# Five of nine tap products summed with help from Pool, smaller tiles for two matmul stages, and one group of the attention loop for each fill

## The chip, the cores and the metric

One Trainium2 chip, one of its cores. The metric is the device time of one execution in microseconds (us). Engines: PE (TensorE), DVE (VectorE), ACT (ScalarE), POOL (GpSimd, "Pool" below) and SP, which issues the transfers.

## The reference

The input x is 4 images of 64 channels x 64 x 64, float32. Three layers follow one another:

1. A dynamic 3x3 filter. conv1 (64 to 16 channels), batch norm and relu, then conv2 (16 to 9) give nine numbers for each pixel; the output is the sum over the nine taps of shifted pixel times (number + bias): `out = einsum('bckhw,bkhw->bchw', patches, wdyn)`. It is reshaped to (4, 4096, 64): 4096 tokens of 64 an image.
2. `h = h + attention(layernorm(h))`, one head of width 64, softmax over 4096 keys.
3. `h = h + ffn(layernorm(h))`: router logits over 32 experts, the first best one, hidden layer of 16 with relu, back to 64, bias, relu.

## The kernel before, in words

**Tiling.** A block is 1024 queries (8 rows of pixels in each half of an image, 128 partitions x 512 numbers). There are 4 blocks to an image (NQ) and 16 in all (BLOCKS). Attention of block n runs over 16 groups (PAIRS) of 256 keys: in group g, PE multiplies scores for two units (`score`, L573), ACT takes the exponential of each unit (L736), and PE weighs the values of group g-1 (`into_z`, L583) into the PSUM tensor z_ps. Both work in 64x64 tiles, four beside one another.

**Fills.** All other work of PE goes in small steps, "fills", that are laid into the groups of the attention loop by a plan written out by hand (`opening_groups` for n=0 and ahead of it, `second_groups` for n=1, `usual_groups` for n=2 to 15, `last_groups` for n=16). Each fill writes a PSUM bank pair called `both` (the nine taps of block 0 use the two banks of z_ps), and another engine drains it before the next fill may write it. `cc`/`cv` are conv1/conv2 of two blocks at once; SP stores the nine numbers to memory (`store_filters`, L309) and loads them back spread over the 64 channels (`spread_filters`, L321), three taps (a chunk) at a time into two slots. `sum0 sum1 sum2` are DVE's alone: per tap one product (L856, `tap`) and, but for tap 0, one add into hres (L861). Behind the ninth tap DVE normalises the block (L824 to L837, writes `keys`). `xt` turns the keys over (L448), `g` multiplies them by the query-key matrix (L513). Behind attention of block m: DVE adds the two halves of z (L1011, L1013), `pz` multiplies by the value matrix (L521, 128x128 tiles), DVE divides and normalises (L918 to L837, writes y_block), `yt` turns, `lg` gives logits (L527, 128x128 tiles), DVE copies and picks (L928 to L943), `ot` turns the picks, `hid0` to `hid3` are the hidden layer (L539, L543, ACT drains at L729), `o2` the second layer (L550, L556), `fin` turns back (L564) and DVE adds the residual (L954); SP stores the block.

**Order.** In group g, each engine does the scores (or exponentials), then the fills of the group in the plan's order, and PE then weighs group g-1. In a usual block n, with m = n-1 behind and i = n+4 ahead: `sum0` in group 0, `cc` in 1 and `cv` in 5 (for every other n only), `sum1` in 2, `pz` in 3, `sum2` in 4, `yt` in 6, `lg` in 7, `fin` of m-1 in 8, `xt` in 9, `ot` in 10, `hid0` in 11, `hid1` and `g` in 12, `hid2` in 13, `hid3` in 14, `o2` in 15. For n from 12 on nothing lies ahead, so `sum`, `xt` and `g` are missing. n=16 is the tail: only the fills behind block 15, with no attention beside them.

**Opening.** Before the first scores: conv1 of block 0 in full, its nine taps one after another on PE (L473) in 32x128 tiles, each drained by DVE straight from PSUM, with six steps of a bound on the scores' size between them (`pow0` to `pow5`, read by ACT and at last by DVE's `judge`), then the layer norm, `xt`, `cc` of blocks 3 and 4, `g`, `cv`. The sums of blocks 1, 2 and 3 follow on DVE during attention of block 0, whose groups 4, 8 and 12 need the keys of each.

`settle()` is a drain of DVE's pipeline between dependent operations. `rsqrt` is three Newton steps on 128x8 numbers. Pool does only set-up: weights, constants (L360 to L417).

## Time and profile before

| | |
|---|---|
| three timed runs, us | 1240.64, 1241.97, 1242.17 (median 1241.97) |
| the profiled execution, its own time | 1238.29 |
| its span, first to last instruction | 1236.2 |
| mean granted clock of PE | 0.984 of 2.4 GHz |
| PE busy | 1156.3 (94%) |
| ACT busy | 623.8 (50%) |
| DVE busy | 496.5 (40%) |
| POOL busy | 10.1 (1%) |
| chain that ended last, by engine | PE 68%, DVE 20%, waits and queues 12% |

Busy is the time in which at least one instruction of the engine ran. The two largest groups of PE are the scores (L573, 506.1 us busy) and the weighing (L583, 506.6 us), which overlap at their edges. The chain is followed back from the last instruction to what released it at each step. In a timeline, a row gives start, length, engine, line, operation, tiles, count (two records for one float32 matmul), and in brackets how long the engine stood idle before it and which instruction it then followed.

### The profile page before, as it was taken

The page shows a single profiled execution, that of the slowest core. Times are in us where ns is not written, and L with a number is a line of the kernel's source. Part 1 is how long each engine was busy: PE and PEld are TensorE (multiplying, and loading weights), DVE is VectorE, ACT ScalarE, POOL GpSimd, SP SyncE. Part 2 cuts the span into 40 slices and gives each one's busy share as a digit, 9 for nine tenths or more (in the row PEclk, how much of TensorE's full clock was granted, in tenths as well). Part 3 has the DMA queues.
Part 4 walks back from the last instruction along what each step waited for, and adds up shares of the span by engine and source line. Part 5 has one row for each costly group of instructions (what it writes and reads, how often), then busy time and mean ns, then how long its engine had stood idle before and what let it go on. Part 6 is the DMA issues. An engine that isn't in the chain of part 4 may idle for free.

```text
span 1236.2 us, 28064 instructions
## 1 busy us (share of the span) xinstructions
PE 1156.3 (94%) x12122; PEld 464.9 (38%) x12122; DVE 496.5 (40%) x1130; ACT 623.8 (50%) x664; POOL 10.1 (1%) x36
## 2 busy tenths in 40 slices
PE   7698999999999999999999999999999999999965
PEld 2133434333343433434343333434334333434431
DVE  4882774518072452707245170724403030313131
ACT  1255555555555455555555555554555555554611
POOL 3000000000000000000000000000000000000000
PEclk9999999999999999999999999999999999999986
DMA  5543231201214120121212012121000000000000
GB/s 139 120 114 89 70 89 27 63 2 31 57 28 98 27 61 1 32 58 28 60 28 55 10 34 54 27 62 27 10 2 10 1 2 10 1 10 1 10 1 18
DMA packets 11886, 48.42 MB, mean 39 GB/s; under 512 B 2462, under 2 KB 2590, under 8 KB 11372
## 3 DMA queue, kind: packets, MB, share of 16 engines
q1 hardware_dynamic: 11756, 46.53, 15.8%
q8 instruction: 101, 1.65, 0.6%
q14 instruction: 29, 0.24, 0.1%
HBM read 41.77 MB, written 4.75 MB: 38 GB/s over the span
## 4 chain that ended last, share of the span: by engine, by line
PE 68%; DVE 20%; DVEq 4%; issue 4%; ACT 2%; DMA 2%; SPq 0%; ACTq 0%
PE z_ps L583 26%; PE scores L573 24%; PE both L556 5%; DVEq L803 4%; PE both L543 4%; DVE hres L861 4%; DVE tap_product L856 2%; PE both L448 1%; PE z_ps L473 1%; DVE tap_product L828 1%; DVE tap_product L826 1%; DVE stat L824 1%; DVE stat L830 1%; DMA filter_ring<-filters 1%; ACT hidden L729 1%
## 5 line engine op out<-in xcount | busy, mean ns | idle before, releaser
L736 ACT ACTIVATE probs<-scores 128x1024 f32<-128x1024 f32 x480 | 465.4, 1021 | 472.7 <-PE scores L573 472.7
L573 PE MATMUL scores<-g_t,keys_t 64*64 64x512 f32 x4096 | 506.1, 592 | 3.1 <-issue 2.9
L583 PE MATMUL z_ps<-probs,keys 64*64 64x512 f32 x4096 | 506.6, 593 | 0.2 <-DVE z_sb L1013 0.2
L573 PEld LDWEIGHTS scores<-g_t,keys_t 64*64 64x64 f32 x4096 | 170.3, 134 | 281.8 <-issue 275.7
L583 PEld LDWEIGHTS z_ps<-probs,keys 64*64 64x64 f32 x4096 | 160.7, 133 | 230.3 <-issue 204.6
L946 DVE COPY o_sb<-both 128x512 f32<-128x512 f32 x16 | 11.1, 692 | 487.0 <-PE both L556 487.0
L861 DVE TENSOR_TENSOR hres<-hres,tap_product 128x504 f32<-128x504 f32 (+1 forms) x128 | 88.0, 688 | 10.8 <-issue 0.5
L856 DVE SCALAR_TENSOR_TENSOR tap_product<-filter_ring,w,xin 128x504 f32<-128x504 f32 (+1 forms) x120 | 89.0, 742 | 6.1 <-DMA filter_ring<-filters 2.2
L729 ACT ACTIVATE hidden<-both 128x1024 f32<-128x1024 f32 x64 | 65.5, 1023 | 10.0 <-PE both L543 10.0
L543 PE MATMUL both<-y_t,w 64*64 64x512 f32 x512 | 70.0, 618 | 0.0
L556 PE MATMUL both<-hidden,w 64*64 64x512 f32 x512 | 66.2, 604 | 0.0
L736 ACT ACTIVATE probs<-scores,first_scale 128x1024 f32<-128x1024 f32 x32 | 34.1, 1111 | 22.7 <-PE scores L573 22.5
L1011 DVE COPY z_sb<-z_ps 128x512 f32<-128x512 f32 x16 | 11.1, 692 | 81.9 <-PE z_ps L583 81.9
L556 PEld LDWEIGHTS both<-hidden,w 64*64 64x64 f32 x512 | 27.1, 136 | 25.0 <-issue 23.6
L513 PE MATMUL both<-keys_t,a_w 64*64 64x512 f32 x128 | 18.2, 639 | 14.7 <-ACT hidden L729 12.6
L539 PE MATMUL both<-onehot_t,mask_w 64*64 64x512 bf16 x256 | 26.3, 392 | 4.2 <-ACT hidden L729 3.4
L543 PEld LDWEIGHTS both<-y_t,w 64*64 64x64 f32 x512 | 20.2, 138 | 22.7 <-issue 18.9
L564 PE MATMUL both<-w,o_sb 64*64 64x64 f32 x512 | 11.3, 228 | 15.3 <-DVE logits L928 13.6
L725 ACT COPY g_t<-both 128x1024 f32<-128x1024 f32 x16 | 16.2, 1012 | 16.7 <-PE both L513 16.7
L448 PE MATMUL both<-w,keys 64*64 64x64 f32 x512 | 10.9, 225 | 13.8 <-DVE keys L837 13.8
L828 DVE TENSOR_TENSOR tap_product<-tap_product 128x512 f32<-128x512 f32 x32 | 22.2, 693 | 2.4
L830 DVE TENSOR_REDUCE stat<-tap_product 128x8 f32<-128x512 f32 x32 | 22.0, 686 | 2.3
(113 smaller groups left out, 542.9 us busy)
## 6 DMA issues: line engine op xcount, KB each, us to landing
filter_ring<-filters SPq DMA_DIRECT2D x90, 384.0 KB, 5.4
out_dram<-out_sb SPq DMA_DIRECT2D x32, 128.0 KB, 2.4
xin<-x_dram SPq DMA_DIRECT2D x6, 528.0 KB, 7.4
hidden<-once_dram SPq DMA_DIRECT2D x1, 930.0 KB, 12.8
hidden<-once_dram SPq DMA_DIRECT2D x1, 576.0 KB, 4.5
filters<-filters_sb SPq DMA_DIRECT2D x30, 18.0 KB
xin<-x_dram SPq DMA_DIRECT2D x1, 384.0 KB, 6.2
xin<-x_dram SPq DMA_DIRECT2D x1, 368.0 KB, 7.3
```

Source lines behind the costliest of these rows:

```text
L539: T.matmul(both[rows_of(c), r, :], mask_w[rows_of(r), f * 128 + 64 * c:f * 128 + 64 * c + 64], onehot_t[rows_of(r), :], start=True, stop=F ...
L543: last = T.matmul(both[rows_of(c), r, :], w1[rows_of(r), f * 128 + 64 * c:f * 128 + 64 * c + 64], y_t[rows_of(r), :], start=False, stop=True)
L556: last = T.matmul(both[rows_of(r), h, :], w2[rows_of(h), f, :], hidden[rows_of(h), f, r, :], start=(f == 0 and h != r), stop=(f == FT - 1))
L573: last = T.matmul(scores[rows_of(h), c, r * 512:(r + 1) * 512], keys_t[rows_of(r), n // NQ % 2, g * 128 + 64 * h:g * 128 + 64 * h + 64], g ...
L583: last = T.matmul(z_ps[rows_of(c), h, :], keys[rows_of(h), n // NQ % 2, 2 * g + r, :], probs[rows_of(h), (2 * g + c) % RING, r * 512:(r + ...
L729: A.activation(hidden[:, int(name[3:]), :, :], both[:, :, :], ACT.Relu).then_inc(done, 1)
L736: A.activation(probs[:, unit % RING, :], scores[:, c, :], ACT.Exp, scale=SCALE if n else first_scale[:, 0:1]).then_inc(probs_ready, 1)
L803: dve.drain()
L828: V.tensor_tensor(squares[:, :, :], centred[:, :, :], centred[:, :, :], ALU.mult)
L830: V.reduce_sum(total, squares[:, :, :], AX_X)
L856: product = V.scalar_tensor_tensor(dst, flt, keep["b2c"][:, t:t + 1], pix, ALU.add, ALU.mult)
L861: V.tensor_tensor(mine[:, :, lo:hi], mine[:, :, lo:hi], dst, ALU.add)
```

## The change

- **Pool sums.** Tap 2's product goes into a new tile pool_sum; the products of taps 3 to 6 go into two buffers in turn, and Pool adds each to pool_sum. DVE waits before a product whose buffer is still to be read, and, behind tap 8, for all four adds of the block, and then adds pool_sum to hres itself. On DVE five adds a block go and one comes. Pool does `add_products(0)` before the rest of its set-up, and the other blocks' after it.
- **Tiles.** `pz` and `lg` go in 64x64 tiles; ACT instead of DVE drains `lg`. The division behind `pz` is one reciprocal instead of two.
- **Groups.** `fin` of m-1 moves from group 8 to 2, `cv` from 5 to 4, `xt` from 9 to 8, `g` from 12 to 9: each fill has a group of its own. In n=1, `xt`, `g` and `sum2` likewise, and `g` of block 5 moves into n=2. `cc` and `cv` of blocks 3 and 4 move out of the opening into groups 1 and 2 of n=0.
- **Opening.** Six PSUM places for the taps of block 0; tap t uses rows 32(t%4) onward of the array, the six first ones go before `cc`/`cv`; the `pow` steps go behind all taps; DVE's small work on row means moves from tap 0 to tap 6; ACT loads its table before the first data are there.
- **Tail.** For block 15, `hid1`, `hid2` and `o2` get PSUM places of their own, and DVE drains one half of each `hid` (a relu as max with 0) while ACT drains the other.

```diff
+POOL_FIRST, POOL_ADDS = 2, (3, 4, 5, 6)
+PLACE_OF_TAP = (4, 0, 1, 2, 3, 5, 6, 7, 8)
...
 def opening_groups():
-
+    first = "tap0 tap1 tap2 tap3 tap4 tap5"
     return {
-        -1: [*at(0, "c1 tap0 tap1 pow0 aw tap2 pow1 tap3 pow2"), *at(1, "cc"), *at(0, "tap4 pow3 tap5 pow4"),
-             *at(1, "cv"), *at(0, "tap6 pow5 tap7 tap8 xt"), *at(3, "cc"), *at(0, "g"), *at(3, "cv")],
+        -1: [*at(0, "c1 " + first), *at(1, "cc cv"),
+             *at(0, "tap6 tap7 tap8 pow0 aw pow1 pow2 pow3 pow4 pow5 xt g")],
         0: at(1, "sum0 sum1 sum2"),
+        1: at(3, "cc"),
+        2: at(3, "cv"),
         3: at(1, "xt"),
         4: [*at(1, "g"), *at(2, "sum0 sum1 sum2")],
...
-    return {3: at(m, "pz"), 6: at(m, "yt"), 7: at(m, "lg"), 8: at(m - 1, "fin"), 10: at(m, "ot"),
+    return {2: at(m - 1, "fin"), 3: at(m, "pz"), 6: at(m, "yt"), 7: at(m, "lg"), 10: at(m, "ot"),
             11: at(m, "hid0"), 12: at(m, "hid1"), 13: at(m, "hid2"), 14: at(m, "hid3"), 15: at(m, "o2")}
...
-    return merged({1: at(j, "cv"), 0: at(i, "sum0"), 2: at(i, "sum1")}, behind(0),
-                  {4: at(i, "sum2"), 8: at(j, "sum0 sum1"), 9: at(i, "xt"), 12: at(i, "g"), 13: at(j, "sum2"),
-                   16: at(j, "xt g")})
+    return merged({0: at(i, "sum0"), 1: at(j, "cv"), 2: at(i, "sum1"), 4: at(i, "sum2")}, behind(0),
+                  {8: [*at(i, "xt"), *at(j, "sum0 sum1")], 9: at(i, "g"), 12: at(j, "sum2"), 16: at(j, "xt")})
 
...
-    pair = at(j, "cc"), at(j, "cv")
-    ahead = {1: pair[0], 5: pair[1]} if j in PAIRED else {}
-    return merged(ahead, {0: at(i, "sum0"), 2: at(i, "sum1"), 4: at(i, "sum2")}, behind(n - 1),
-                  {9: at(i, "xt"), 12: at(i, "g")})
+    ahead = {1: at(j, "cc"), 4: at(j, "cv")} if j in PAIRED else {}
+    return merged({0: at(NQ + 1, "g")} if n == 2 else {}, ahead,
+                  {0: at(i, "sum0"), 2: at(i, "sum1"), 4: at(i, "sum2")}, behind(n - 1),
+                  {8: at(i, "xt"), 9: at(i, "g")})
...
+                    k = FIRST_TAP + int(name[3:]) % TAP_PLACES if name.startswith("tap") else USUAL
+                    if i == BLOCKS - 1:
+
+                        k = LAST.get(name, USUAL)
...
+        score_banks = [scores[:, c, :].rearrange("p (u n) -> p u n", u=2) for c in range(2)]
+        place = [both, *(score_banks[c][:, u, :] for c in range(2) for u in range(2)), z_ps[:, 0, :], z_ps[:, 1, :],
+                 *score_banks, z_ps]
...
+            def add_products(i):
+                for k, t in enumerate(POOL_ADDS):
+                    nth = i * len(POOL_ADDS) + k
+                    lo, hi = columns_of(t)
+                    pool.wait_ge(product_ready, nth + 1)
+                    P.tensor_tensor(pool_sum[:, :, lo:hi], pool_sum[:, :, lo:hi], pool_product[:, nth % 2, :, lo:hi],
+                                    ALU.add).then_inc(product_added, 1)
+                    pool.drain()
...
+            for i in range(1, BLOCKS):
+                add_products(i)
...
-                    T.matmul(scores[0:DB, 0, 0:DB], centred_qk[:, 0, :], centred_qk[:, 1, :], start=True,
+                    wait_drained("tap4@0")
+                    T.matmul(z_ps[0:DB, 0, 0:DB], centred_qk[:, 0, :], centred_qk[:, 1, :], start=True,
...
-                    T.matmul(mine, load["w2c"][0:32, t * 128:(t + 1) * 128], conv1_first[:, :], start=True,
+
+                    rows = slice(32 * (t % 4), 32 * (t % 4) + 32)
+                    T.matmul(mine, load["w2c"][rows, t * 128:(t + 1) * 128], conv1_first[rows, :], start=True,
                              stop=True).then_inc(done, 1)
...
-                    for p in range(2):
-                        for j in range(2):
-                            jj = 2 * p + j
-                            last = T.matmul(both[:, p, j * 130:(j + 1) * 130], z_sb[:, jj * 128:(jj + 1) * 128],
-                                            wv_w[:, :], start=True, stop=True)
+                    for j in range(BT // 2):
+                        for c in range(2):
+                            for h in range(2):
+                                last = T.matmul(both[rows_of(h), c, j * 65:(j + 1) * 65],
+                                                z_sb[rows_of(c), j * 128 + h * 64:j * 128 + h * 64 + 64],
+                                                wv_w[rows_of(c), c * 65:(c + 1) * 65], start=True, stop=True)
...
-                        last = T.matmul(mine[:, j * 64:(j + 1) * 64], y_t[:, j * 128:(j + 1) * 128],
-                                        router_w[:, :], start=True, stop=True)
+                        for r in range(2):
+                            for h in range(2):
+                                last = T.matmul(both[rows_of(h), r, j * E:(j + 1) * E],
+                                                y_t[rows_of(r), j * 128 + h * 64:j * 128 + h * 64 + 64],
+                                                router_w[rows_of(r), :], start=True, stop=True)
...
+                    if i == BLOCKS - 1 and f == FT - 1:
+                        pe.wait_ge(upper_hidden, 1)
...
+                        if i == BLOCKS - 1:
+                            pe.wait_ge(upper_hidden, f + 1)
...
+                elif name == "lg":
+                    A.copy(logits[:, :, :].rearrange("p (j r) e -> p r j e", r=2),
+                           both[:, :, 0:BT // 2 * E].rearrange("p r (j e) -> p r j e", e=E)).then_inc(done, 1)
...
-                    A.activation(hidden[:, int(name[3:]), :, :], both[:, :, :], ACT.Relu).then_inc(done, 1)
+
+                    mine_of = slice(0, 1 if i == BLOCKS - 1 else 2)
+                    A.activation(hidden[:, int(name[3:]), mine_of, :], mine[:, mine_of, :], ACT.Relu).then_inc(done, 1)
...
+            act.wait_ge(constants_ready, 1)
+            A.activation(table_loaded[:, :], ones[0:1, 0:1], ACT.Relu)
...
+            def first_best(i):
+
+                dve.wait_ge(drained[places.of[f"lg@{i}"]], places.nth[f"lg@{i}"])
...
-                dst = mine if t == 0 else tap_product[:, t % 2, :, lo:hi]
+                if t == 0:
+                    dst = mine
+                elif t == POOL_FIRST:
+
+                    dst = pool_sum[:, :, :]
+                elif t in POOL_ADDS:
+                    nth = i * len(POOL_ADDS) + t - POOL_ADDS[0]
+                    dst = pool_product[:, nth % 2, :, lo:hi]
+                    if nth > 1:
+                        dve.wait_ge(product_added, nth - 1)
+                else:
+                    dst = tap_product[:, t % 2, :, lo:hi]
                 product = V.scalar_tensor_tensor(dst, flt, keep["b2c"][:, t:t + 1], pix, ALU.add, ALU.mult)
                 if sources_free is not None:
                     product.then_inc(sources_free, 1)
                 settle()
-                if t:
+                if t in POOL_ADDS:
+                    V.engine_nop().then_inc(product_ready, 1)
+                elif t and t != POOL_FIRST:
                     V.tensor_tensor(mine[:, :, lo:hi], mine[:, :, lo:hi], dst, ALU.add)
+                if t == TAPS - 1:
+                    dve.wait_ge(product_added, (i + 1) * len(POOL_ADDS))
+                    settle()
+                    V.tensor_tensor(mine, mine, pool_sum[:, :, :], ALU.add)
 
             def judge():
...
+                if name == "lg":
+                    first_best(i)
+                    return
+                if name.startswith("hid") and i == BLOCKS - 1:
+                    f, k = int(name[3:]), places.of[full]
+                    dve.wait_ge(filled[k], places.nth[full])
+                    V.tensor_scalar(hidden[:, f, 1, :], place[k][:, 1, :], 0.0, None, ALU.max).then_inc(upper_hidden, 1)
+                    return
...
                 if full == "tap0@0":
                     dve.wait_ge(x_first_loaded, 32)
+                if full == "tap6@0":
...
-                    sums = both[:, :, 0:260].rearrange("p u (j a w) -> p u j a w", j=2, a=2)
-                    rs = stat[:, 4, :].rearrange("p (u j a) -> p u j a", u=2, j=2)
-                    rows = h2[:, i % 2, :, :].rearrange("p (u j a) w -> p u j a w", u=2, j=2)
-                    for u in range(2):
-                        V.reciprocal(rs[:, u], sums[:, u, :, :, D])
-                        settle()
-                        last = V.tensor_tensor(rows[:, u], sums[:, u, :, :, 0:D], wide(rs[:, u], D), ALU.mult)
+                    sums = both[:, :, 0:BT // 2 * 65].rearrange("p a (j w) -> p a j w", w=65)
+                    rs = stat[:, 4, :].rearrange("p (a j) -> p a j", a=2)
+                    rows = h2[:, i % 2, :, :].rearrange("p (j a) w -> p a j w", a=2)
+                    V.reciprocal(rs, sums[:, :, :, D])
+                    settle()
+                    for a in range(2):
+                        last = V.tensor_tensor(rows[:, a], sums[:, a, :, 0:D], wide(rs[:, a], D), ALU.mult)
                     last.then_inc(done, 1)
```

## Rows read from the trace of the kernel before

**Rows 1.** Windows: span, then busy us (instructions) by engine, granted clock, DMA.

```profile
960.00:1040.00 80.00, 79.76 (x836) 31.45 (x832) 13.67 (x35) 44.75 (x47) 0.00 (x0) 1.00 0.02 5
...
1200.00:1210.00 10.00, 5.39 (x108) 4.73 (x112) 3.54 (x9) 1.17 (x2) 0.00 (x0) 0.50 0.06 15
```

**Rows 2.** Timeline, DVE, two attention blocks; columns: start, us, engine, line, operation, idle before.

```profile
417.30 0.69 DVE L1011 COPY z_sb<-z_ps 128x512 f32<-128x512 f32 x1 [3.69 <-PE z_ps L583]
...
423.98 0.68 DVE L861 TENSOR_TENSOR hres<-hres,tap_product 128x504 f32<-128x504 f32 x1
424.58 0.74 DVE L856 SCALAR_TENSOR_TENSOR tap_product<-filter_ring,w,xin 128x504 f32<-128x504 f32 x1
...
446.75 0.68 DVE L837 TENSOR_TENSOR keys<-tap_product,stat 128x504 f32<-128x504 f32 x1
...
450.53 0.75 DVE L954 SCALAR_TENSOR_TENSOR out_sb<-both,h 128x256 f32<-128x256 f32 x2
...
499.60 0.18 DVE L918 RECIPROCAL stat<-both 128x4 f32<-128x4 f32 x1 [0.68 <-PE both L521]
```

**Rows 3.** Timeline, PE, the first of those two blocks.

```profile
447.82 0.69 PE L564 MATMUL both<-w,o_sb 64*64 64x64 f32 x32 [1.83 <-DVE logits L928]
...
466.48 1.09 PE L513 MATMUL both<-keys_t,a_w 64*64 64x512 f32 x8 [1.14 <-ACT hidden L729]
```

**Rows 4.** Timeline, PE, a late block, where no later block is prepared.

```profile
995.77 1.90 PE L573 MATMUL scores<-g_t,keys_t 64*64 64x512 f32 x16
...
998.68 1.95 PE L583 MATMUL z_ps<-probs,keys 64*64 64x512 f32 x16
...
1009.50 1.90 PE L583 MATMUL z_ps<-probs,keys 64*64 64x512 f32 x16
1011.22 1.90 PE L573 MATMUL scores<-g_t,keys_t 64*64 64x512 f32 x16
...
1014.08 1.95 PE L583 MATMUL z_ps<-probs,keys 64*64 64x512 f32 x16
```

**Rows 5.** Timeline, DVE and POOL in the opening.

```profile
13.39 0.74 DVE L856 SCALAR_TENSOR_TENSOR tap_product<-z_ps,w,xin 128x504 f32<-128x504 f32 x1 [0.96 <-PE z_ps L473]
13.54 0.23 POOL L394 CAST b_bf<-b_rest 32x64 bf16<-32x64 f32 x1
14.23 0.68 DVE L861 TENSOR_TENSOR hres<-hres,tap_product 128x504 f32<-128x504 f32 x1
14.33 0.67 POOL L398 CAST b_bf<-b_rest 32x64 bf16<-32x64 f32 x1
...
19.55 0.41 POOL L408 TENSOR_TENSOR wv_w<-hidden 128x130 f32<-128x130 f32 x1 [2.40 <-DMA hidden<-once_dram]
19.58 0.92 DVE L861 TENSOR_TENSOR hres<-hres,tap_product 128x504 f32<-128x504 f32 x1
...
21.14 1.26 POOL L413 TENSOR_TENSOR w<-hidden 128x512 f32<-128x512 f32 x1
```

**Rows 6.** Timeline of the opening, and the page's line of filter loads.

```profile
14.23 2.07 PE L473 MATMUL z_ps<-conv_first,hidden 32*128 32x512 f32 x2
...
41.71 0.68 DVE L837 TENSOR_TENSOR keys<-tap_product,stat 128x504 f32<-128x504 f32 x1
...
52.56 4.69 PE L573 MATMUL scores<-g_t,keys_t 64*64 64x512 f32 x24
...
55.36 31.56 SPq L321 DMA_DIRECT2D filter_ring<-filters  x12
...
101.96 0.68 DVE L837 TENSOR_TENSOR keys<-tap_product,stat 128x504 f32<-128x504 f32 x1
...
filter_ring<-filters SPq DMA_DIRECT2D x90, 384.0 KB, 5.4
```

**Rows 7.** Timeline, PE, behind the last attention block.

```profile
1213.44 0.64 PE L539 MATMUL both<-onehot_t,mask_w 64*64 64x512 bf16 x4 [1.14 <-ACT hidden L729]
...
1223.94 0.64 PE L550 MATMUL both<-onehot_t,b_parts 64*64 64x512 bf16 x2 [1.15 <-ACT hidden L729]
```

More of the change, by code:

```diff
@@ L295, in store_block @@
                 fin = f"fin@{m}"
[L296 removed]
+                sp.wait_ge(drained[places.of[fin]], places.nth[fin])
                 for half in range(HH):
@@ L461, in fill @@
                 wait_free(full)
-                k = banks_of.sem[full]
-                mine, done = banks[k], filled[k]
+                k = places.of[full]
+                mine, done = place[k], filled[k]
                 par, q = i // NQ % 2, i % NQ
@@ L698, in drain @@
                     act.wait_ge(a_written, 1)
-                    A.copy(a_w[:, :], scores[:, 1, 0:128]).then_inc(a_ready, 1)
+                    A.copy(a_w[:, :], z_ps[:, 1, 0:128]).then_inc(a_ready, 1)
                 if name.startswith(NONE) or not name.startswith(MINE):
                     return
-                k = banks_of.sem[full]
-                mine, done = banks[k], drained[k]
+                k = places.of[full]
+                mine, done = place[k], drained[k]
                 turned = both[:, :, 0:BT // 2 * 64].rearrange("p h (j n) -> p h j n", n=64)
```

154 lines of the change are left out of this document (74 added, 80 removed).

## The prediction

> **What bounds the kernel now.** I read the windows first, then PE's timeline of one block, then DVE's. In a late block PE is busy for 79.76 of 80 us at the full 2.4 GHz level, DVE for 13.67 [rows 1]: PE's own work is the bound there, and only work taken off PE counts. In the blocks that prepare a later one it is not. There PE stands 1.83 us before `fin`, because the bank still holds logits that DVE copies only after it has normalised the keys (end 447.43, copy, `fin` at 447.82), and 1.14 us before `g`, which shares its group with `hid1` and waits for ACT [rows 3]. In these blocks DVE's chain from the copy of z (417.30) to the end of the keys (447.43) is 30.1 us long [rows 2] and sets when PE leaves group 8. Behind the last attention block PE works for 5.39 of 10 us with granted clock 0.50, the 1.2 GHz level [rows 1]: a chain of fills and drains. The opening is a DVE chain too: keys of block 0 at 42.39, of block 3 at 102.64, so 20.1 us for each block between [rows 6].
>
> The sum is made against the profiled execution, 1238.3 us (span 1236.2 and 2.1 around it). The median of the runs is 1242.0, so it lies 3.7 higher, and so I place the forecast. What can be told from no change is about 0.2%, 2.5 us.
>
> **Pool's adds (n=2 to 11).** The question is whether they run beside DVE. Pool's cast of 32x64 takes 0.23 us beside a DVE product that reads PSUM, but 0.67 when it starts 0.10 us into a DVE add of two SBUF tensors, and ends 0.09 behind that add; and a DVE add that begins inside a Pool operation takes 0.92 instead of 0.68 [rows 5]. So they shut each other out, at least in large part. A Pool add of this size is 1.26 us (L413) [rows 5]. DVE's two read-from-SBUF operations are most of what it does in `sum`.
>
> The Trainium skill (SBUF — State Buffer, SBUF: two separate sides) says that a GpSimd operation and a DVE operation with two SBUF inputs lock each other out for the whole instruction. By it four adds would cost 4 x 1.26 = 5.0 us of DVE's time a block wherever DVE had such work. The trace agrees in kind, not quite in size: DVE lost 0.24 us to 0.38 of overlap, 0.63 of it, which would make the four adds 3.2 us.
>
> DVE's chain in such a block, change by change:
> - five adds go, each worth 0.60, the step from its start to the next product [rows 2]: -3.0;
> - one add of pool_sum with its drain comes: +0.8;
> - `fin`'s drain (0.75, L954 [rows 2]) moves ahead of `pz`: +0.75; one reciprocal of 0.18 and its drain go: -0.25;
> - tap 3's add: DVE waits for it before tap 5, 1.26 and some 0.15 of signalling: +1.4;
> - adds of taps 4 and 5: between 0 (they lie beside the drains of `fin` and `pz`, which read PSUM, and beside DVE's wait for `pz`) and 2.6 (Pool gets in before DVE's products, and `fin`, then `pz`, come late); nearest to the first by where they fall: +1.0;
> - tap 6's add falls between products of two SBUF tensors: 1.26, taken as +1.3.
>
> Together +2.0: keys later, not earlier. `xt` now stands in group 8 where `fin` was, so PE waits there for the keys: about 0.2 behind them, at 449.6 where `fin` began at 447.82 before: +1.8. Against this one fill of 0.5 fewer follows (`fin` is done in group 2), and `g` no longer waits (-1.14). Net +0.1. The time saved on `pz` and `lg` is no gain here, since PE waits in group 8 anyhow. In every other block (those with `cc`, `cv`) DVE had waited 0.68 for `pz` [rows 2], which absorbs as much of the +2.0, and PE stood there for less before; with the rest of the same sum about -1.1. Ten blocks: **-5 us**. n=1 likewise: 0. Without any exclusion only the wait of 0.6 before tap 5 remains of the Pool terms, the chain is 1.1 shorter, less what `pz` lets through, and each block gains 2.7: -27. With every add at its worst (+1.6 more) the ten blocks give +11.
>
> **Late blocks (n=12 to 15).** `pz` takes 998.68 - 995.77 - 1.72 = 1.19 us and `lg` 1014.08 - 1011.22 - 1.72 = 1.14, where 1.72 is the step of 16 records of scores or values [rows 4]. In 64x64 tiles each is 16 matmuls, like a turning fill, about 0.5; `fin`, also of 16, is 0.69 with its tail [rows 3]. -0.7 and -0.7, and each had 0.05 of change-over behind it. **-5.8** for four blocks; if the narrower `lg` is quicker still, -6.5. `fin` moved to group 2 costs nothing: DVE is free then. Its place is used again by `pz` one group later, DVE's drain (0.75) lies beside 3.4 us of scores and values.
>
> **Opening.** Before, PE makes a tap in 2.07 us at the low clock [rows 6] and DVE waits 0.96 for it [rows 5]. With six places and four row groups I take four taps in the time of one: two rounds (4 us), `cc`/`cv` with ACT between (5.5), a third round (2). DVE's keys of block 0 then come at about 31, `judge` behind them, and block 1 starts at 32.6 instead of 42.6 (0.2 behind the keys); first scores at 36.5 instead of 52.56. But SP's queue is in order: `store_filters(3)`, then block 2's loads, issued at 55.36 before [rows 6]. `cv` of block 3 is now in group 2, behind two groups' exponentials, drained at about 49. The loads go out at 50.5 and take 5.4 each [rows 6]: block 2 starts at 56 instead of 62.7 (-6.7), and waits 2 us more for its second chunk. Within a block the third chunk can be loaded only when the first is used, and comes 8.8 us after the block's start with fewer adds as with more, so those saved before it give nothing; Pool's adds around it cost about 2 us in each of two blocks. **-1 us** of the 10 that block 1 gains. Without exclusion -5. No trace here shows 32-row tiles beside one another; if they go one by one, keys 0 come only 2 us earlier, the loads of block 2 land at 65, and the opening gives +6.5.
>
> **Tail.** The hidden fills come every 3.50 us, from 1213.44 to 1223.94 [rows 7], and 1.15 of each is PE's wait for ACT. With places of their own they follow one another: 4 x 1.15 = -4.6. PE then has no gaps, and I expect it to reach the 2.4 GHz level before `o2`: between 0 and -4.5, taken as -2.5. `fin` of block 14 goes from between `lg` and `ot` (0.75 of DVE) to under `pz`, which it delays by 0.75; `lg` at the low clock saves 0.8 and `ot` no longer follows `fin`: together about -1.9. **-9 us** (-6 to -11).
>
> **Sum.** -5 - 0 - 5.8 - 1 - 9 = -21: 1217 for a profiled execution, 1220 for the median.
>
> **The rivals.**
> - *Pool's adds are hidden* (0.18). Then -27 - 2 (n=1) - 5.8 - 5 - 9 = -49: 1193. For it: DVE lost less than the full overlap; against it: all three crossings in [rows 5].
> - *Pool's add is the slow link* (0.12). On 8 rows of 63 in a running kernel, with its wait, drain and signal, it may take longer than the 1.26 of a plain 128x512. About three of four adds are on DVE's chain in each of ten blocks, n=1 and two of the opening. From 0.55 us more for each, 1.8 in all, the gain of 21 is used up; at 2.5 us (twice) the sum is -21 + 13 x 3 x 1.24 = +27: 1269. Against it: the one clean row.
> - *Row tiles don't overlap* (0.10): opening +6.5 instead of -1, 1228.
> - The sum as above (0.60): 1220, own range 1207 to 1232.
>
> Faster by over 0.2% is 0.83: the sum, hidden adds, row tiles. Within 0.2%: 0.05, slower 0.12, both from the slow link. The range reaches down to the hidden adds' 1193 and up past the row tiles' case: 1192 to 1240.
>
> **What would show it.** Right: DVE operations of two SBUF inputs stretched or held off beside Pool's adds; Pool busy about 64 x 1.26 = 81 us; PE idle 1 to 4 us before `xt` in each block to n=11 with keys as releaser, none before `fin` and `g`; `pz` and `lg` steps of 0.5; hidden fills of the tail without gaps; block 2's first product after a DMA wait. Wrong: no wait before `xt` (adds hidden, or DVE chain shorter), Pool adds well above 1.3 us, late blocks no shorter, or PE stalls before `pz` for `fin`'s drain longer than 1.3 us.

## The result, and the profile after

The changed kernel takes **1224.46 us** (1223.57 to 1224.93), the kernel before 1241.5 in the same session: a ratio of 0.9861, 95% interval 0.9841 to 0.9880. A fourth execution took 1981.72 us at a mean granted clock of 0.567; it counts in this median, which is 1223.99 without it, but not in the range or the ratio. The forecast was 1220. The profiled execution took 1224.93, with a span of 1223.1 where it was 1236.2 before: 13.1 shorter. The medians differ by 17.0, more than the spans, since the profiled execution of before (1238.29) lay 3.2 under that kernel's median; what follows compares the two traces.

I cut both spans at DVE's copies of z (L1011 before, L1078 after), one at the end of each attention block:

| stretch (us) | before | after | difference | predicted |
|---|---|---|---|---|
| start to z of n=0, and n=1 | 200.81 | 204.21 | +3.4 | -1 |
| n=2 to 11, ten blocks | 720.83 | 721.38 | +0.6 | -5 |
| n=12 to 14 | 201.48 | 196.92 | -4.6 | -4.4 |
| n=15 and the tail | 113.08 | 100.59 | -12.5 | -10.5 |

So the four rows add up to -13 instead of -21. The stretches without Pool's adds gave what was forecast or more, those with them 10 us less.

First the page after: busy time of each engine, PE's granted clock in 40 slices (tenths of full speed), three groups of instructions.

```profile
PE 1130.4 (92%) x12890; PEld 478.8 (39%) x12890; DVE 467.2 (38%) x1038; ACT 626.6 (51%) x681; POOL 114.8 (9%) x98
...
PEclk9989899999999999999999999999999999999996
...
L377 POOL TENSOR_TENSOR pool_sum<-pool_sum,pool_product 128x504 f32<-128x504 f32 x64 | 104.2, 1628 | 750.0 <-DVEq L931 744.9
L469 PE MATMUL both<-w,keys 64*64 64x64 f32 x512 | 15.2, 277 | 54.6 <-DVE keys L879 54.6
...
L933 DVE TENSOR_TENSOR hres<-hres,tap_product 128x504 f32<-128x504 f32 (+1 forms) x48 | 46.9, 976 | 3.9
```

Pool's 64 adds take 1.63 us in the mean, not 1.26. DVE's own add (L933) takes 0.98 in the mean where one took 0.68 [rows 2]. PE stands 54.6 us before `xt` (L469), and one record of `xt` takes 277 ns in the mean.

DVE and POOL in the steady block that answers to [rows 2], where before the same chain ran from 417.30 to 447.43 (timeline; start, us, engine, line, operation, idle before):

```profile
421.43 0.69 DVE L1078 COPY z_sb<-z_ps 128x512 f32<-128x512 f32 x1 [3.69 <-PE z_ps L616]
...
427.18 1.79 POOL L377 TENSOR_TENSOR pool_sum<-pool_sum,pool_product 128x504 f32<-128x504 f32 x1 [54.79 <-DVEq L931]
429.01 0.74 DVE L926 SCALAR_TENSOR_TENSOR pool_product<-filter_ring,w,xin 128x504 f32<-128x504 f32 x1 [1.15 <-POOL pool_sum L377]
...
441.16 1.82 POOL L377 TENSOR_TENSOR pool_sum<-pool_sum,pool_product 128x504 f32<-128x504 f32 x1 [8.86 <-DVEq L931]
441.93 1.60 DVE L933 TENSOR_TENSOR hres<-hres,tap_product 128x512 f32<-128x512 f32 x1
...
451.78 0.68 DVE L879 TENSOR_TENSOR keys<-tap_product,stat 128x504 f32<-128x504 f32 x1
```

The chain is 452.46 - 421.43 = 31.0 us, 0.9 longer than before. DVE waits 1.15 for Pool's first add, and an add of DVE that meets one of Pool's takes 1.60.

PE behind the same keys, then in the next block, answering to [rows 3]:

```profile
452.61 1.13 PE L469 MATMUL both<-w,keys 64*64 64x64 f32 x32 [3.05 <-DVE keys L879]
453.49 3.05 PE L616 MATMUL z_ps<-probs,keys 64*64 64x512 f32 x16
456.35 1.90 PE L606 MATMUL scores<-g_t,keys_t 64*64 64x512 f32 x16
...
525.03 0.69 PE L469 MATMUL both<-w,keys 64*64 64x64 f32 x32 [2.20 <-DVE keys L879]
525.51 1.93 PE L616 MATMUL z_ps<-probs,keys 64*64 64x512 f32 x16
527.23 1.93 PE L606 MATMUL scores<-g_t,keys_t 64*64 64x512 f32 x16
```

and the windows around both (span, busy us of PE, PEld, DVE, ACT, POOL, granted clock, DMA share, GB/s):

```profile
452.00:456.00 4.00, 3.39 (x48) 1.81 (x52) 2.83 (x7) 0.59 (x1) 0.00 (x0) 0.57 0.00 0
...
524.00:528.00 4.00, 2.97 (x56) 1.62 (x60) 3.17 (x8) 0.59 (x1) 0.00 (x0) 1.00 0.02 4
```

Behind the wait of 3.05 us the granted clock is 0.57, so mostly the 1.2 GHz level: `xt` and the weighing take 456.35 - 452.61 = 3.74 us where behind the wait of 2.20 they take 527.23 - 525.03 = 2.20. In this pair **1.5 us are lost to the clock**, on top of the wait; waits of 3.05 to 3.42 stand in every block without `cc` and `cv`. The waits before `fin` and before `g` are gone, as forecast.

A late block's `pz`, answering to [rows 4]:

```profile
998.65 1.90 PE L606 MATMUL scores<-g_t,keys_t 64*64 64x512 f32 x16
1000.37 0.64 PE L545 MATMUL both<-wv_w,z_sb 64*64 64x65 f32 x32
1000.83 1.90 PE L616 MATMUL z_ps<-probs,keys 64*64 64x512 f32 x16
```

From scores to weighing it is 2.18, so `pz` costs 2.18 - 1.72 = 0.46.

The opening, PE's taps of block 0, then SP's queue and DVE's first product of block 2, answering to [rows 6]:

```profile
8.57 2.09 PE L497 MATMUL scores<-conv_first,hidden 32*128 32x512 f32 x8 [1.02 <-ACT conv_first L745]
...
32.34 0.68 DVE L879 TENSOR_TENSOR keys<-tap_product,stat 128x504 f32<-128x504 f32 x1
...
50.80 1.35 SPq L320 DMA_DIRECT2D filters<-filters_sb  x4
52.26 2.37 SPq L332 DMA_DIRECT2D filter_ring<-filters  x4
...
58.33 0.75 DVE L926 SCALAR_TENSOR_TENSOR hres<-filter_ring,w,xin 128x512 f32<-128x512 f32 x1 [3.24 <-DMA filter_ring<-filters]
...
100.52 0.68 DVE L879 TENSOR_TENSOR keys<-tap_product,stat 128x504 f32<-128x504 f32 x1
```

Four taps (8 records) take 2.09 us, where one took 2.07 before. Keys of block 0 come 9.4 us earlier, keys of block 3 only 1.4 earlier. And then PE, at the change from n=0 to n=1:

```profile
118.67 1.90 PE L616 MATMUL z_ps<-probs,keys 64*64 64x512 f32 x16
122.95 1.93 PE L606 MATMUL scores<-g_t,keys_t 64*64 64x512 f32 x11 [2.38 <-issue]
125.99 1.12 PE L606 MATMUL scores<-g_t,keys_t 64*64 64x512 f32 x3 [1.11 <-issue]
...
126.92 3.61 PE L616 MATMUL z_ps<-probs,keys 64*64 64x512 f32 x12
```

From 124 to 131 us the granted clock is 0.55, so PE works mostly at the low level (12 records in 3.61). Before, a stop of 2.20 at this place was followed by full speed (granted clock 1.00 from 120 to 130 us), and z was copied at 128.39 instead of 131.50.

The tail, answering to [rows 7]:

```profile
1206.21 0.64 PE L570 MATMUL both<-onehot_t,mask_w 64*64 64x512 bf16 x4 [0.79 <-ACT onehot_t L764]
1206.61 1.95 PE L574 MATMUL both<-y_t,w 64*64 64x512 f32 x8
...
1208.74 1.73 PE L574 MATMUL scores<-y_t,w 64*64 64x512 f32 x8
...
1212.88 3.61 PE L589 MATMUL z_ps<-hidden,w 64*64 64x512 f32 x30
```

No gaps between the hidden fills; the full clock is back in the second hidden fill (8 records in 1.73 where the first has 1.95, and 30 in 3.61 for `o2`).

### The profile page after: what moved, and what is told of

It reads as the page before. It is cut to its first block, busy times and chain, and to the rows that moved or that the text cites. A ratio compares the mean times of both kernels' runs of the same rounds, so it can differ in the third digit from the quotient of the medians.

```text
span 1223.1 us, 29732 instructions
## 1 busy us (share of the span) xinstructions
PE 1130.4 (92%) x12890; PEld 478.8 (39%) x12890; DVE 467.2 (38%) x1038; ACT 626.6 (51%) x681; POOL 114.8 (9%) x98
## 4 chain that ended last, share of the span: by engine, by line
issue 61%; PE 26%; POOLq 9%; DVE 3%; DVEq 0%; POOL 0%; DMA 0%; ACT 0%
PE z_ps L616 10%; PE scores L606 10%; POOLq L379 8%; PE both L574 2%; PE both L589 1%; PE both L469 1%; PE both L570 0%; PE z_ps L589 0%; PE both L545 0%; DVEq L845 0%; PE both L554 0%; PE both L597 0%; PE scores L574 0%; DVE hres L933 0%; DVE tap_product L870 0%
## 5 line engine op out<-in xcount | busy, mean ns | idle before, releaser
L616 PE MATMUL z_ps<-probs,keys 64*64 64x512 f32 x4096 | 521.0, 605 | 0.5 <-issue 0.2
L606 PEld LDWEIGHTS scores<-g_t,keys_t 64*64 64x64 f32 x4096 | 181.6, 135 | 277.4 <-issue 266.9
L616 PEld LDWEIGHTS z_ps<-probs,keys 64*64 64x64 f32 x4096 | 173.4, 137 | 227.2 <-issue 198.3
L1013 DVE COPY o_sb<-both 128x512 f32<-128x512 f32 x15 | 10.4, 692 | 469.5 <-PE both L589 469.5
L377 POOL TENSOR_TENSOR pool_sum<-pool_sum,pool_product 128x504 f32<-128x504 f32 x64 | 104.2, 1628 | 750.0 <-DVEq L931 744.9
L469 PE MATMUL both<-w,keys 64*64 64x64 f32 x512 | 15.2, 277 | 54.6 <-DVE keys L879 54.6
L768 ACT ACTIVATE hidden<-both 128x1024 f32<-128x1024 f32 (+1 forms) x62 | 62.6, 1010 | 3.0 <-PE both L574 3.0
L926 DVE SCALAR_TENSOR_TENSOR pool_product<-filter_ring,w,xin 128x504 f32<-128x504 f32 x60 | 45.3, 756 | 32.7 <-POOL pool_sum L377 17.3
L933 DVE TENSOR_TENSOR hres<-hres,tap_product 128x504 f32<-128x504 f32 (+1 forms) x48 | 46.9, 976 | 3.9
L1078 DVE COPY z_sb<-z_ps 128x512 f32<-128x512 f32 x16 | 11.1, 692 | 85.0 <-PE z_ps L616 85.0
L755 ACT COPY keys_t<-both 128x512 f32<-128x512 f32 x16 | 9.4, 587 | 59.2 <-PE both L469 59.2
L469 PEld LDWEIGHTS both<-w,keys 64*64 64x64 f32 x512 | 12.9, 181 | 67.5 <-issue 66.7
L926 DVE SCALAR_TENSOR_TENSOR tap_product<-filter_ring,w,xin 128x504 f32<-128x504 f32 (+1 forms) x45 | 33.4, 742 | 3.0
```

The lines of the kernel that those rows point to most:

```text
L377: P.tensor_tensor(pool_sum[:, :, lo:hi], pool_sum[:, :, lo:hi], pool_product[:, nth % 2, :, lo:hi], ALU.add).then_inc(product_added, 1)
L469: last = T.matmul(both[rows_of(a), h, j * 64:(j + 1) * 64], tiles[2 * j + a][rows_of(h)], ident[rows_of(h), rows_of(h)], start=True, stop= ...
L606: last = T.matmul(scores[rows_of(h), c, r * 512:(r + 1) * 512], keys_t[rows_of(r), n // NQ % 2, g * 128 + 64 * h:g * 128 + 64 * h + 64], g ...
L616: last = T.matmul(z_ps[rows_of(c), h, :], keys[rows_of(h), n // NQ % 2, 2 * g + r, :], probs[rows_of(h), (2 * g + c) % RING, r * 512:(r + ...
L768: A.activation(hidden[:, int(name[3:]), mine_of, :], mine[:, mine_of, :], ACT.Relu).then_inc(done, 1)
L926: product = V.scalar_tensor_tensor(dst, flt, keep["b2c"][:, t:t + 1], pix, ALU.add, ALU.mult)
```

## The experiments

Two questions: what do Pool's adds cost, and where did the 8 us go. In the first theory Pool was neutral (it costs DVE about what it takes off DVE); its rivals were that its adds are a net loss or a net gain. A time that is given as so much below or above the changed kernel is against its 1224.46.

**Pool out.** DVE adds all eight products itself.

```diff
-                if t in POOL_ADDS:
-                    V.engine_nop().then_inc(product_ready, 1)
-                elif t and t != POOL_FIRST:
+                if t:
...
-                    V.tensor_tensor(mine, mine, pool_sum[:, :, :], ALU.add)
```

> The changed kernel, but DVE adds all eight products itself again and Pool adds none. Theory A (Pool's adds and DVE's operations on two SBUF tensors shut each other out, so that the adds taken off DVE come back as waits and stretched operations): DVE's chain from the copy of z to the end of the keys stays within 0.5 us of the 31.0 us that it has with Pool, the blocks n=2 to 11 stay as long as they are, and the opening gains some 2 us; 1219 to 1226 us, ratio to the kernel before 0.984 +- 0.003. Rival B (Pool relieves DVE, the loss lies elsewhere): the chain gets 2 us longer, each of ten blocks too, 1240 us or more, ratio about 1.0.

Measured 1205.92 (ratio 0.9719, 0.9702 to 0.9735): 18.5 below the changed kernel. Both expectations missed. Yet the chain from z to keys, by the ten blocks n=2 to 11, is 31.3 us in the mean against 31.5 with Pool and 30.4 before: Pool is neutral for DVE there, and the ten blocks are still 10.6 us shorter, 9.1 of it between the end of the keys and the next copy of z. Another 11.6 us go before z of n=1, and there Pool is not neutral: keys of block 3 come 65.1 us after those of block 0 without it, 68.2 with it. The trace of n=5, the block of the first pair above:

```profile
416.15 0.70 PE L542 MATMUL both<-wv_w,z_sb 64*64 64x65 f32 x32 [1.47 <-DVE out_sb L1004]
...
437.18 0.69 PE L466 MATMUL both<-w,keys 64*64 64x64 f32 x32 [2.23 <-DVE keys L876]
437.67 2.74 PE L613 MATMUL z_ps<-probs,keys 64*64 64x512 f32 x12
```

Without Pool, DVE comes later to `fin`'s drain, so PE stands 1.47 before `pz` (0.26 with Pool) and then only 2.23 before `xt`. The same idle time is cut in two, and `xt` takes 0.69. This block is also the exception: right behind `xt` the clock falls even so (0.60 granted from 437 to 441 us), and it takes 41.3 from keys to the next copy of z. In the nine others that is 39.6 to 39.9, with waits of 1.0 to 2.2 before `xt`. In the changed kernel it is 39.6 behind four of the five waits of 2.2 to 2.6, and 40.9 to 42.5 behind the fifth of them and behind all five of 3.05 to 3.42. That made the clock the new theory.

**`xt` one group later**, with Pool and without (`xt` in group 9, `g` in 16).

```diff
-                  {8: at(i, "xt"), 9: at(i, "g")})
+                  {9: at(i, "xt"), 16: at(i, "g")})
```

> The changed kernel with xt in group 9 instead of 8 and g in group 16 instead of 9, for n=2 to 15. Theory A (what ate the gain is PE's wait for the keys in group 8, 2.2 to 3.4 us in each of ten blocks, and the lower clock behind the longer of these waits, about 1.5 us in every other block): one group later (3.4 us) the wait is gone and the granted clock stays high there; 10 x 2.75 + 5 x 1.5 = 35 us less, about 1190, ratio 0.958. Rival B (DVE's chain bounds the block wherever xt stands: PE waits for the picks before ot, or before pz): less than 10 us gained, ratio above 0.978.

> Both edits: xt in group 9, g in 16, and no adds on Pool. Theory A (Pool's adds are neutral for DVE's chain): within 4 us of the kernel with xt later and Pool's adds, rather below it through the opening; 1184 to 1192 us. Rival B (Pool's adds are what makes room for DVE): over 5 us slower than that kernel, waits before xt come back.

Measured 1196.64 with Pool (0.9636, 0.9620 to 0.9652), 27.8 less where the theory had 35, and 1196.74 without (0.9641, 0.9625 to 0.9657): within the 4 us of each other that were forecast, but above the 1184 to 1192. The waits for keys fall from 15 (54.6 us) to 5 (26.6) with Pool, and PE waits for no keys in n=2 to 11 in either. The equal times hide two differences that cancel. Up to z of n=1 it takes 202.5 us with Pool and 194.3 without; the ten blocks take 695.2 with Pool and 702.0 without, and there PE stands 1.6 us before `pz` with Pool and 11.3 without, since DVE with all its adds comes later to `fin`'s drain. So in this pair Pool's adds gain in the steady blocks, once the wait for the keys is out of the way, and about as much is lost before them. In both runs three image changes show a new stop, behind `g`'s drain; with Pool:

```profile
611.60 1.09 PE L537 MATMUL both<-keys_t,a_w 64*64 64x512 f32 x8
615.42 3.11 PE L606 MATMUL scores<-g_t,keys_t 64*64 64x512 f32 x16 [2.73 <-issue]
```

**Work added into the wait.** The direct test of the clock: eight matmuls of 64x512 in each block n=2 to 11, whose result `xt` overwrites. Eight float32 matmuls are 16 records; the expectation, and the next one, give the count of records.

```diff
+                        if 6 <= i < BLOCKS:
+                            for _ in range(2):
+                                for r in range(2):
+                                    for c in range(2):
+                                        T.matmul(both[rows_of(c), r, :], a_w[rows_of(r), rows_of(c)],
+                                                 keys_t[rows_of(r), 1 - par, 0:512], start=True, stop=True)
                         pe.wait_ge(xn_ready, i + 1)
```

> The changed kernel with 16 matmuls of 64x512 more in each of the blocks n=2 to 11, ahead of PE's wait for the keys: they overwrite the place that xt fills right behind and are read by nobody. Theory (the 3.05 to 3.42 us wait before xt makes the granted clock fall, the 2.2 to 2.6 us wait doesn't, and the fall costs 1.5 us each time): the 1.7 us of added work lies in the wait, what is left of it is 1.3 to 1.7, xt takes 0.69 everywhere instead of 1.13, and from the keys to the next copy of z it is 39.6 in every block instead of 41.1 to 41.6 in every second one: 1224.5 - 6 x 1.5 = 1215 to 1217, faster by more work. Rival (what is lost in these blocks is the waiting itself or something else beside it, not the clock): 1224 to 1225, with 41.1 as before.

Measured **1212.42** (0.9760, 0.9742 to 0.9777): 12 us less time with more work, more than expected. PE in the block that answers to the first pair above:

```profile
444.76 1.90 PE L531 MATMUL both<-keys_t,a_w 64*64 64x512 f32 x16
447.91 0.70 PE L469 MATMUL both<-w,keys 64*64 64x64 f32 x32 [1.25 <-DVE keys L885]
448.43 1.90 PE L622 MATMUL z_ps<-probs,keys 64*64 64x512 f32 x16
```

The added row is L531. The granted clock from 447 to 451 us is 1.00, where behind the same keys it was 0.57. DVE's chains are what they were (31.04 here, 31.03 in the changed kernel), and from keys to the next z it is 39.5 to 39.7 in all ten blocks. The ten blocks take 709.82 instead of 721.38, -11.6, without touching Pool, DVE or the order of the fills. The theory holds. It had counted 6 falls at 1.5 us; five of them were worth 1.4 to 2.1 (8.3 together), and the one in n=11 3.0.

**The same in the opening**: also before `xt` of blocks 2 and 3 (12 matmuls, 24 records, each) and 4 (8 and 16).

```diff
-                        if 6 <= i < BLOCKS:
-                            for _ in range(2):
+                        if 2 <= i < BLOCKS and i != 5:
+                            for _ in range(3 if i < 4 else 2):
```

> The kernel of k_filler with the added matmuls also ahead of xt of blocks 2 and 3 (24 each, 2.6 us at full clock, in waits of 7.7 and 4.3) and of block 4 (16, in a wait of 3.4). Theory (what the opening lost to the kernel before from xt of block 3 to the first o2, 6 us, is granted clock that falls behind these waits and at the image's end): xt of blocks 3 and 4 at 0.69, the weighing behind xt of block 3 at 1.9 instead of 2.9, PE at full clock at the first change of the query block (120 to 131 us), copy of z there at 127 to 128 instead of 130.6: 1212.4 - 4 to 6 = 1206 to 1208. Rival (the fall at the change of the block comes from its own stop of 2.3 us, whatever was before it): xt at 0.69 but the half-clock stretch of 120 to 131 stays, 1210 to 1212.

Measured **1206.98** (0.9727, 0.9703 to 0.9751), 5.4 less again. PE at the change to n=1, with the stop still there:

```profile
121.60 1.95 PE L612 MATMUL scores<-g_t,keys_t 64*64 64x512 f32 x16 [2.33 <-issue]
123.34 1.93 PE L622 MATMUL z_ps<-probs,keys 64*64 64x512 f32 x16
```

Against the run before this one, z of n=0 is copied at 125.40, not 130.55, and the granted clock of 120 to 130 us is 1.00 instead of 0.83. So the stop of 2.3 us alone doesn't bring the clock down; it did in company with what lay before it. With added work in its waits the changed kernel reaches 1207.0, where taking Pool out gave 1205.9: in total nearly all of the 18 us that Pool seemed to cost can be had back without touching Pool. By stretches the two are not alike: up to z of n=1 it is 196.6 us here and 192.7 without Pool, and the ten blocks take 709.5 here and 710.8 there.

**Pool's lock by itself.** The kernel before, with Pool working on a scratch buffer: 14 adds beside block 1's sums, 14 copies beside block 2's, 22 memsets beside block 3's, and 24 adds from pv_done 17. That semaphore counts groups, so the last series of adds (a "train") ran in n=1, not in late blocks; of late blocks this run says nothing.

```diff
+            pool.wait_ge(xn_ready, 1)
+            for _ in range(14):
+                P.tensor_tensor(probe[:, 0, :], probe[:, 1, :], probe[:, 2, :], ALU.add)
+                pool.drain()
```

> The kernel before, with Pool work on a scratch buffer that nobody reads: 14 adds of two 128x512 SBUF tensors from the moment block 0's keys are done (beside the sums of block 1), 14 plain copies of 128x512 beside those of block 2, 22 memsets beside those of block 3, and 24 adds beside the late blocks. Theory (the two engines exclude each other for whole instructions, when DVE has two SBUF operands): DVE's add of 0.68 stands at 1.2 to 1.9 in many records beside Pool's adds, the sums of block 1 get at least 5 us longer, Pool's own add goes from 1.26 alone to above 1.7 in the mean, and DVE operations with a PSUM operand keep their times. Rival (they share bandwidth): every DVE operation, those from PSUM too, is stretched by the same 10 to 30%, none to twice its time. If copies and memsets of Pool don't take part, DVE's records in blocks 2 and 3 are as before. In late blocks, where DVE is 17% busy, the time doesn't move.

Measured 1276.85, one execution, against 1240.44. By the traces nearly all of the difference lies beside Pool's work: 18.8 us up to z of n=0 and 19.4 in n=1, while each block from n=2 to 15 is as long as before. DVE in the first train, at its end, and beside Pool's last train:

```profile
62.71 1.60 DVE L883 TENSOR_TENSOR hres<-hres,tap_product 128x504 f32<-128x504 f32 x1
64.23 1.75 DVE L878 SCALAR_TENSOR_TENSOR tap_product<-filter_ring,w,xin 128x512 f32<-128x512 f32 x1
66.06 0.69 DVE L883 TENSOR_TENSOR hres<-hres,tap_product 128x512 f32<-128x512 f32 x1
...
163.74 0.42 DVE L942 TENSOR_TENSOR h<-both,stat 128x256 f32<-128x256 f32 x1
...
165.61 0.69 DVE L846 TENSOR_REDUCE stat<-h 128x8 f32<-128x512 f32 x1
166.38 0.84 DVE L848 SCALAR_TENSOR_TENSOR tap_product<-stat,h 128x512 f32<-128x512 f32 x1
167.30 1.60 DVE L850 TENSOR_TENSOR tap_product<-tap_product 128x512 f32<-128x512 f32 x1
```

In the first train every DVE operation with two SBUF inputs alternates with one Pool add: an add takes 1.60 instead of 0.68, so **0.91 us for each Pool add**. From block 0's keys to block 1's it takes 32.5 us instead of 20.1, so 12.4 more, where at least 5 were forecast; Pool's add took 1.53 (median), stretched from 1.26 but under the 1.7 expected. An operation that reads PSUM (0.42) and a reduce of one tensor (0.69) aren't touched. Not everything with one tensor is spared: in the last train a TENSOR_SCALAR of 128x8, 0.17 alone, took 1.08 at 170.38 us, and an add that started at the same moment as Pool's (164.85) kept its 0.69. The groups of DVE's products by form, in the windows of the copies and of the memsets, show that the kind of Pool's work matters:

```profile
L878 DVE SCALAR_TENSOR_TENSOR tap_product<-filter_ring,w,xin 128x504 f32<-128x504 f32 x5 | 5.0, 990 | 0.2
...
L878 DVE SCALAR_TENSOR_TENSOR tap_product<-filter_ring,w,xin 128x504 f32<-128x504 f32 x6 | 4.4, 740 | 0.8 <-DMA filter_ring<-filters 0.7
```

0.25 more beside copies, nothing beside memsets, which read nothing. So the two engines exclude each other, though not in the same way for every kind of Pool's work: a copy takes part after all, if little. Bandwidth shared in proportion is refuted, since operations that read PSUM keep their times.

**The tail's places undone.** The last hidden fills share the usual place again, ACT drains them alone.

```diff
-USUAL, FIRST_TAP, TAP_PLACES, LAST = 0, 1, 6, {"hid1": 7, "hid2": 8, "o2": 9}
+USUAL, FIRST_TAP, TAP_PLACES, LAST = 0, 1, 6, {}
```

> The changed kernel with the last block's hidden fills in the one usual place again, drained by ACT alone. Theory (each fill waits 1.15 us for ACT's drain, and these gaps also hold PE at the low clock up to o2): 1224.5 + 7, with hidden fills every 3.5 us and o2 at 0.50 of the clock: 1231 to 1233. Rival one (waits only, the clock rises by itself behind the onehot step): +4.6, 1229. Rival two (the whole tail gain of 11 us measured is from these places): 1235.

Measured 1231.65 (0.9918, 0.9900 to 0.9936), +7.2, the theory's number. Its trace, the longest of its four executions, has more: from `ot` (at 1202.71 in it, at 1204.29 in the changed kernel) to the end 29.2 us instead of 18.8, so +10.4. Waits are 4.6 of that,

```profile
1211.62 0.64 PE L568 MATMUL both<-onehot_t,mask_w 64*64 64x512 bf16 x4 [1.15 <-ACT hidden L764]
```

and the other 5.8, what is left, goes with the clock, granted at 0.50 up to 1220 us where the changed kernel has 0.89 from 1210 on. By the median the places are worth 7.2, by this trace 10.4; by either the clock's part is at least the 2.5 that I had taken.

**Filter loads first.** Block 2's loads ahead of the wait for block 3's.

```diff
-            store_filters(3)
             spread_filters(2)
+            store_filters(3)
             spread_filters(3)
```

> The changed kernel with SP's loads of block 2's filters ahead of the wait for block 3's, two lines exchanged. Theory (block 2's sums wait for SP's queue, which waits for cv of block 3 to be drained at 50 us): the first product of block 2 comes at 55 instead of 58.3, limited then by keys of block 1 at 55.1, keys of block 2 some 3 us earlier, and the time 1221 to 1222. Rival (what is gained goes again behind block 3's keys, in PE's half-clock stretches at 102 and 119 us): 1224 to 1225.

Measured 1219.88 (0.9833, 0.9818 to 0.9849), -4.6. Block 2's first product moves from 58.33 to 54.60, right behind block 1's keys, and keys of blocks 2 and 3 both come 3.9 earlier. More than the theory gave.

**`pz` in 128x128 tiles again** (8 records instead of 32, two reciprocals).

```diff
-                                last = T.matmul(both[rows_of(h), c, j * 65:(j + 1) * 65],
-                                                z_sb[rows_of(c), j * 128 + h * 64:j * 128 + h * 64 + 64],
-                                                wv_w[rows_of(c), c * 65:(c + 1) * 65], start=True, stop=True)
+                            last = T.matmul(both[:, p, j * 130:(j + 1) * 130], z_sb[:, jj * 128:(jj + 1) * 128],
+                                            wv_w[:, :], start=True, stop=True)
```

> The changed kernel with the value matmuls (pz) in four 128x128 tiles again, and the two reciprocals with them; lg stays in 64x64 tiles. The prediction held that pz's 0.7 us is no gain in the blocks n=2 to 11, since PE waits in group 8 anyhow: then only the four late blocks and the tail pay, 4 x 0.7 + 0.5 = +3 us over the changed kernel (1228). Rival: in the changed kernel DVE waits for pz in every block, so pz is a link of the chain that ends in the wait before xt, and each of ten blocks pays 0.7 and the second reciprocal's 0.25 as well: +12 to +13 us (1237).

Measured 1231.77 (0.9917, 0.9900 to 0.9934), +7.3. A late block takes 66.30 instead of 65.64 in the mean, so four of them 2.7, the 0.7 for each `pz` that the forecast took. In n=2 to 11 DVE's chain is 0.7 longer too (32.2 in the mean), because `pz` is filled that much later, and PE waits for its end: seven more in ten blocks, where the theory had nothing. Together that is 9.8, by the median it is 7.3, between theory and rival. Its trace, the longest of five executions, has the ten blocks 8.4 longer, 7.1 by the chain and the rest behind the keys. It also has two waits that go against a plain rule of length, in n=3 and in n=8:

```profile
309.63 0.69 PE L469 MATMUL both<-w,keys 64*64 64x64 f32 x32 [3.09 <-DVE keys L878]
...
672.65 2.84 PE L615 MATMUL z_ps<-probs,keys 64*64 64x512 f32 x16
```

Behind the wait of 3.09 the granted clock stays at 1.00 (309 to 314 us), and behind one of 2.61 it is 0.66 (672 to 677), with a weighing of 2.84.

**A version that beats both.** Pool out, `xt` in 9, `g` in 15, `o2` in 16, loads first.

```diff
+    tail = behind(n - 1)
+    tail[16] = tail.pop(15)
...
-                  {8: at(i, "xt"), 9: at(i, "g")})
+                  {9: at(i, "xt"), 15: at(i, "g")})
```

> The changed kernel with Pool's adds taken out (DVE adds all eight), xt in group 9, g in group 15, the o2 of the block behind in group 16 instead of 15, and SP's loads of block 2 first. Theory (with xt in 9 and g in 16 the three image changes each leave PE 4 us without work behind g's drain, which ACT makes only after its exponentials; DVE drains o2 at once): 1196.7 - 12 - 3 = 1182, range 1178 to 1186, windows of the image changes back at 67.6 to 69 us between the o2 of two blocks. Rival (the gap is the image change itself): 1193 to 1196. A third way: g in 15 makes PE wait for ACT there in every block, as before in group 12: 1196 or more.

Measured **1181.41** (0.9521, 0.9507 to 0.9534), in the range forecast (1178 to 1186); the gaps at the image changes are gone. What it still waited for was `fin`'s drain before `pz`, 12.9 us in ten blocks. So, one step further:

```diff
-    ahead = {1: at(j, "cc"), 4: at(j, "cv")} if j in PAIRED else {}
+    ahead = {0: at(j, "cc"), 4: at(j, "cv")} if j in PAIRED else {}
...
+    tail[1] = tail.pop(2)
```

> The kernel of i_best with fin of the block behind in group 1 instead of 2, ahead of DVE's second chunk of sums, and cc in group 0 to make room. Theory (with all adds on DVE, PE stands 1.3 us before pz in each of ten blocks, since DVE comes to fin's drain only behind the second chunk): those 12.9 us of waits go and nothing waits anew, 1181.4 - 12 = 1169 to 1171. Rival (cc in group 0 meets the place's earlier owner or ACT's exponentials, or the drain of fin now holds the chunk and the keys come late): waits before fin, cc or xt take what pz gives, 1178 to 1182.

Measured **1168.56** (1167.95 to 1170.21; 0.9412, 0.9396 to 0.9427), 73 us below the kernel before. Neither of these two was run with Pool's adds in it, so what they would do there is open. The waits of these two, as the list of PE's waits has them, first of i_best, then of this one (in total, times, longest):

```profile
PE both L544 <- DVE out_sb L1006: 12.9, 10, 1.8
```

```profile
PE both L545 <- DVE out_sb L1007: 1.6, 1, 1.6
```

## Why the prediction was right, and where its steps were off

The time (1224.5 for 1220; the terms as written, with the 3.7 for the median, give 1221) lies in the range and the sign is right. Two terms were too favourable, by 5.6 us (ten blocks) and 4.4 (opening), and the tail gave 2 back. That it came so near is in part luck: a loss that the sum didn't have, the clock's, met gains that it didn't have either.

- **Pool's adds: the mechanism right, the size too high.** I had four adds at 3.7 together (1.4, 1.0, 1.3) and DVE's chain +2.0. The chain grew by 1.05 (31.5 against 30.4, ten blocks). In the block shown the adds cost it a wait of 1.15 and one operation stretched by 0.91, 2.1 together: one add that meets DVE costs 0.91, not 1.26, and two of four fell beside `fin`, `pz` and DVE's wait for it, where they cost nothing. The Trainium skill (SBUF — State Buffer, SBUF: two separate sides) says that the pair of ports is held for the whole instruction, and only against a GpSimd operation that reads SBUF. The memsets agree with the second half. On the first, the alternation of 1.60-us operations agrees that they exclude each other, but DVE is held up for 0.91 of Pool's 1.26, not for all; here the measurement decides.
- **The step that failed: "PE waits there for the keys ... Net +0.1" in the ten blocks.** It priced the wait before `xt` by its length alone. I had PE idle 1 to 4 us there and was right (2.2 to 3.4), but behind six of these ten waits the granted clock fell, as it did not behind the two shorter ones before `fin` and `g` [rows 3]. The run with added work prices that at 11.6 us in the ten blocks; without it they would have come out 11 below before, and the -5 would have been exceeded. The term missing was the clock, and it is twice the miss of 5.6. The rest was paid for by the five blocks without `cc` and `cv`: with the clock's part gone they are 1.0 shorter than before, not 0.1 longer, since DVE's chain grew by 1.1 there and not by 2.0. The five others came out at -1.2 for the -1.1 forecast.
- **A step that was wrong and did no harm: "The time saved on `pz` and `lg` is no gain here, since PE waits in group 8 anyhow."** PE waits, but for the end of DVE's chain, and `pz` is a link of that chain: with `pz` in wide tiles and its second reciprocal again, the chain is 0.7 longer in each of the ten blocks.
- **The opening: -1 forecast, +3.4 measured.** Keys of block 3 came 1.4 earlier, for 1 forecast, so SP's queue was read rightly, each step of it 1 to 2 us late: keys of block 0 at 33.0 for 31, loads at 52.3 for 50.5, block 2 at 58.3 for 56. What followed was missing: the clock behind `xt` of block 3 and through the change to n=1. With added work in the waits z of n=0 comes at 125.4, 3.0 before the kernel before.
- **Late blocks: right.** 65.64 a block instead of 67.16 (n=12 to 14, by the table), 1.5 for the 1.45 forecast; `pz` at 0.46 for 0.5.
- **Tail: -9 forecast, -11.** From z of n=15 to the end it takes 36.8 instead of 47.8. The waits are the 4.6 of the sum; the clock, taken as 2.5, is what was too low, 5.8 by one trace. That trace has 5.84 for the 30 records of `o2` where the kernel before had 4.82, so against the kernel before the clock's part is nearer 4.8, an estimate.
- **Rivals.** Hidden adds: refuted by the exclusion. Pool's add as a slow link: it takes 1.63 in the mean, 0.37 more, under the 0.55 from which it would have decided. Row tiles one by one: refuted, 2.09 for four taps. The rival that came closest to happening wasn't on the list: small waits merged into one behind which the clock falls.

## What to carry to other kernels

A wait of PE has two prices: its length, and what the clock takes behind it. In this kernel two smaller waits mostly cost their length; merged into one of 3.05 they cost about 1.5 us more, so a change that tidies small waits away can lose by it. Look in the windows for granted clock under 1.00 behind each wait before you cost it; and if the wait must stay, put work that nobody reads into it and see whether the time falls.

An add given to Pool costs DVE nothing beside work that reads PSUM, and 0.91 us beside products of SBUF tensors, where it gives back what it takes. And compare two kernels stretch by stretch: the pair with `xt` later agrees to 0.1 us in total and differs by 7 and 8 in its parts.

## What the hardware showed that was not expected

- Adding eight matmuls of 64x512 to each of ten blocks made the kernel 12 us faster.
- The wait's own length doesn't decide alone. Full clock followed waits of 3.03 (opening of the kernel before, `xt` took 0.69) and 3.09 (wide `pz`, n=3); a fallen clock followed waits of 2.23 (without Pool, n=5) and 2.61 (wide `pz`, n=8). And the same wait of 2.56 in n=2 was followed by 41.2 us from keys to z in the changed kernel and by 39.6 in the one with the filter loads first. What else counts stays open.
- Pool's copy of 128x512 costs a DVE product 0.25 us and a memset nothing, where an add costs 0.91.
